# A graph network kernel on one core: the edges' states stay in SBUF from the first stage to the second attention

## What is computed

```python
h = relu(layernorm(x)) ; h = relu(h @ W_in + b_in)
for l in range(2):                       # L0: transformer convolution, 4 heads of 32
    res = h
    q, k, v = h@Wq[l]+bq[l], h@Wk[l]+bk[l], h@Wv[l]+bv[l];  e = edge_weight @ We[l]
    a   = softmax over the edges of one target of (q[dst] . (k[src]+e)) / sqrt(32)
    out = segment_sum((v[src] + e) * a, dst);  x_r = h @ Wskip[l] + bskip[l]
    b   = sigmoid([out, x_r, out - x_r] @ Wbeta[l]);  h = b*x_r + (1-b)*out
    h = relu(batchnorm(h)) + res         # statistics over all 50,000 nodes
x = x + h
# L1: for each edge an MLP of (x[src], edge_attr), mean over each target, then for each node an MLP
```

## Time and profile before

| | us |
|---|---|
| median of 3 runs | 2521.9 (2516.4 to 2528.1) |
| the profiled execution, whole | 2527.1 |
| the profiled execution, first to last instruction (its span) | 2525.3 |
| `first_layer_in` | 27 to 553 |
| `attention(0)` | 553 to 803 |
| `batch_norm_params(0)` | 803 to 814 |
| `dense_second` | 814 to 1212 |
| `attention(1)` | 1212 to 1567 |
| `dense_last` | 1576 to 2126 |
| `edge_last` | 2126 to 2525 |

### The profile page before, as it was taken

How to read it: one execution, slowest core, us unless ns; L and a number is a source line. 1 busy time by engine, 2 the same in 40 slices (tenths; PEclk the granted TensorE clock), 3 DMA queues, 4 the chain that set the end, 5 groups by cost and what they waited for, 6 DMA issues and landing times. The chain is left out here.

```text
span 2525.3 us, 38804 instructions
## 1 busy us (share of the span) xinstructions
PE 2013.4 (80%) x7514; PEld 1160.2 (46%) x7514; DVE 1733.3 (69%) x5020; ACT 1371.6 (54%) x2609; POOL 1290.4 (51%) x1119
## 2 busy tenths in 40 slices
PE   0898889879795777778366796499999995799997
PEld 0444444434232444444133232377777774466665
DVE  3899999965797777778422798477777773454552
ACT  0888888862121666666122221477667763556552
POOL 4645554418830333333587000677777763577773
PEclk9999999989797999999677798699999998899999
DMA  4778888859232999999544132999999993434440
GB/s 142 227 245 252 251 256 256 254 178 271 63 92 74 342 360 359 361 368 367 159 122 103 50 90 66 262 293 302 303 305 300 303 290 117 104 95 115 110 111 21
DMA packets 316448, 526.75 MB, mean 209 GB/s; under 512 B 87187, under 2 KB 189472, under 8 KB 316199
## 3 DMA queue, kind: packets, MB, share of 16 engines
q1 hardware_dynamic: 266100, 492.30, 61.5%
q0 software_dynamic: 46400, 33.03, 6.2%
q10 hardware_dynamic: 3824, 0.13, 0.1%
HBM read 304.11 MB, written 221.80 MB: 208 GB/s over the span
## 5 line engine op out<-in xcount | busy, mean ns | idle before, releaser
L476 POOL DMA_INDIRECT first_x<-in_x,first_index x200 | 254.5, 1272 | 230.1 <-ACT first_xn L339 140.8
L339 ACT ACTIVATE first_xn<-first_x,first_nb,first_rstd 125x128 f32<-125x128 f32 x600 | 245.4, 485 | 63.8 <-DVE first_nb L525 63.8
L795 POOL DMA_INDIRECT second_entry<-node_map,second_si x100 | 128.0, 1280 | 258.8 <-DVE second_src_row L808 221.0
L1086 PE MATMUL last_psH<-last_g,W2a 128*128 128x500 f32 x400 | 197.5, 618 | 31.9 <-DVE last_hid L1048 31.9
L868 PE MATMUL second_psZ<-second_h,gate_h 128*128 128x500 f32 x200 | 108.5, 624 | 112.8 <-DVE second_y L820 85.8
L1095 PE MATMUL last_psO<-W2b,last_hid 128*125 128x128 f32 x1600 | 193.3, 275 | 0.0
L1119 POOL DMA_INDIRECT elast_x<-x_rows,elast_si x100 | 138.6, 1386 | 99.8 <-issue 96.6
L1095 PEld LDWEIGHTS last_psO<-W2b,last_hid 128*125 128x125 f32 x1600 | 185.3, 190 | 0.9 <-issue 0.9
L585 PE MATMUL first_psZ<-first_h,gate_h 128*128 128x500 f32 x250 | 131.4, 607 | 47.6 <-DVE first_y L546 46.1
L339 ACT ACTIVATE last_xn<-last_x,last_nb,last_rstd 125x128 f32<-125x128 f32 x400 | 164.0, 486 | 0.1
L577 PE MATMUL first_psW<-first_h,W_in 128*128 128x500 f32 x300 | 157.6, 608 | 0.0
(11 more groups left out here) (260 smaller groups left out, 5326.1 us busy)
## 6 DMA issues: line engine op xcount, KB each, us to landing
hT<-first_h SPq DMA_DIRECT2D x100, 250.0 KB, 3.4
yT<-first_y SPq DMA_DIRECT2D x100, 250.0 KB, 3.5
second_yin<-yT SPq DMA_DIRECT2D x50, 500.0 KB
second_hin<-hT SPq DMA_DIRECT2D x50, 500.0 KB
yT<-second_y SPq DMA_DIRECT2D x50, 500.0 KB
last_yin<-yT SPq DMA_DIRECT2D x50, 500.0 KB
first_x<-in_x SPq DMA_DIRECT2D x100, 224.0 KB
h_rows<-second_rows SPq DMA_DIRECT2D x50, 448.0 KB
```

Of the source, the lines that this page charges most:

```text
L339: last = act.activation(xn[:, j], x[:, j], ACT.Relu, bias=nb[:, j:j + 1], scale=rstd[:, j:j + 1])
L476: pool.indirect_dma_start(x[:, to % X, j], None, a["x"], bass.IndirectOffsetOnAxis(index[:, end, r % 2, j:j + 1], 0), bounds_check=NODES - ...
L795: pool.indirect_dma_start(entry[:, q], None, scratch.node_map, bass.IndirectOffsetOnAxis(si[:, q], 0), bounds_check=NODES - 1, oob_is_err= ...
L1086: last = pe.matmul(psH[h][:, 0:CH], w.W2a[:, 0, h * 128:(h + 1) * 128], g[:, q % 2], start=True, stop=True)
```

## The change

1. Two tiles, `hd` and `hs`, 25 chunks each, are allocated once for `prepare` to `attention(1)`. `first_layer_in` makes the states of the edges' ends right in them and stores them no more; `attention` loads them no more. The map of node numbers (`ident_map`) lies in a part of `hd` until it is stored, so DVE waits once, at round 12, for that store.
2. `attention` writes `yd` over `hs[:, k]`, in place of the ring `yn`. `ydT` and `hdT` are stored in `attention(1)` alone, `hdT` in its query part, for `dense_last`.
3. In `attention`, what DVE made ahead of its first `product` is made in pieces between the products (`prepare(k)`, `count(k)`).
4. `dense_second` reads `yd` and `hd` in SBUF and updates `hd` in place; `load_edges` issues two DMAs, `store_edges` two. `load_edges(c)` waits for the statistics of edge chunk c-2. `ehw`, `eactw`, `eyw2` and `eywn` lie in `eyw`; `eact` and `esig` are single buffers.
5. The rings of `dense_second` shrink: `h2` and `rows` from eight chunks to four (two pairs), `y` from eight to six (three pairs); `yin` and `hin` stay at eight.
6. `dense_second` is written out without a loop (`unrolled`).

```diff
+def unrolled(n, ring, stages):
+    for t in range(n + max(lag for lag, _ in stages)):
+        for lag, stage in stages:
+            if 0 <= t - lag < n:
+                stage(t - lag, (t - lag) % ring, (t - lag) // ring)
...
@@ first_layer_in @@
+        def h1_of(k):
+            q, r = k % U, k // U
+            return h1[:, q] if q < DST else (edge.hd if q == DST else edge.hs)[:, r]
...
                 def store_h(k):
                     q = k % U
-                    table = scratch.hT if q < DST else scratch.hdT if q == DST else scratch.hsT
-                    hold(sp, ph.seen, *h1_made(k))
-                    sp.dma_start(cols_of(table, chunk(k)), h1[:, q]).then_inc(h1_stored[q], 16)
+                    if q < DST:
+                        hold(sp, ph.seen, *h1_made(k))
+                        sp.dma_start(cols_of(scratch.hT, chunk(k)), h1[:, q]).then_inc(h1_stored[q], 16)
...
@@ dense_second @@
-        h2 = ph.sb("h2", [128, U, CH])
-        rows = ph.sb("rows", [TILE, U, TILES, D])
+        h2 = ph.sb("h2", [128, 4, CH])
+        rows = ph.sb("rows", [TILE, 4, TILES, D])
-        y = ph.sb("y", [128, U, CH])
+        y = ph.sb("y", [128, 6, CH])
...
                 def load_edges(c, s, r):
-                    hold(sp, ph.seen, e.ywn, made(c - 2))
-                    sp.dma_start(eyn[:, s], cols_of(scratch.ydT, e_col(c))).then_inc(e_loaded[s], 16)
-                    sp.dma_start(ehd[:, s], cols_of(scratch.hdT, e_col(c))).then_inc(e_loaded[s], 16)
-                    sp.dma_start(eyw[:, s], cols_of(scratch.ywT, e_col(c))).then_inc(e_loaded[s], 16)
-                    sp.dma_start(econt[:, s], run_row(scratch.ct, e_col(c) + 1)).then_inc(e_loaded[s], 16)
+                    hold(sp, ph.seen, e.ywstats, made(c - 2))
+                    sp.dma_start(eyw[:, s], cols_of(scratch.ywT, at(c) * CH)).then_inc(e_loaded[s], 16)
+                    sp.dma_start(econt[:, s], run_row(scratch.ct, at(c) * CH + 1)).then_inc(e_loaded[s], 16)
                 def store_edges(c, s, r):
-                    hold(sp, ph.seen, e.hn, made(c))
-                    sp.dma_start(cols_of(scratch.hdT, e_col(c)), ehn[:, s]).then_inc(ehn_stored[s], 16)
                     hold(sp, ph.seen, e.rows, made(c))
...
                 def make_rows(k, q, r):
-                    act.wait_ge(rows_stored[q // 2], 16 * r + 16)
+                    act.wait_ge(rows_stored[k // 2 % 2], 16 * (k // 4) + 16)
...
                 def make_h2(k, q, r):
-                    dve.wait_ge(m.xz, made(k - U))
+                    dve.wait_ge(m.xz, made(k - 4))
+                    dve.wait_ge(m.turned, made(k - 4))
...
                 def make_y(k, q, r):
-                    dve.wait_ge(m.ystats, made(k - U))
-                    dve.wait_ge(y_stored[q // 2], 16 * r + 16)
+                    dve.wait_ge(m.ystats, made(k - 6))
+                    dve.wait_ge(y_stored[k // 2 % 3], 16 * (k // 6) + 16)
...
                 def edges_h(c, s, r):
+                    dve.wait_ge(e.bnw, made(c))
+                    dve.tensor_tensor(eyw[:, s], eyw[:, s], hd[:, at(c)], ALU.add).then_inc(e.hw, 1)
                     dve.wait_ge(e.bn, made(c))
+                    dve.wait_ge(e.hw, made(c))
+                    dve.tensor_tensor(hd[:, at(c)], eact[:], hd[:, at(c)], ALU.add).then_inc(e.hn, 1)
...
@@ attention, SP @@
-                    sp.dma_start(hd[:, k], cols_of(scratch.hdT, k * CH)).then_inc(in_loaded[q], 16)
-                    if l == 0:
-                        sp.dma_start(hs[:, k], cols_of(scratch.hsT, k * CH)).then_inc(in_loaded[q], 16)
+                def store_hd(k):
+                    sp.dma_start(cols_of(scratch.hdT, k * CH), hd[:, k]).then_inc(hd_stored, 16)
-                steps(C, [(0, load_index), (0, load), (0, load_weights_wide)])
+                steps(C, [(0, load_index), (0, load_weights_wide)] + [(0, store_hd)] * l)
-                steps(C, [(0, load_weight), (0, load_cont), (4, store)])
+                steps(C, [(0, load_weight), (0, load_cont)] + [(4, store_yd)] * l)
...
@@ attention, DVE: one piece of the former preparation behind each product @@
+                    elif 10 <= k < 15:
+                        c = 5 * (k - 10)
+                        after(dve.tensor_tensor(sel[:, c:c + 5], w.blocks[:].rearrange("p (o m) -> p o m", o=1).to_broadcast([128, 5, 128]),
+                                                ind[:, c:c + 5].rearrange("p (c o) -> p c o", o=1).to_broadcast([128, 5, 128]), ALU.mult))
-                steps(C, [(0, product)])
+                steps(C, [(0, product), (0, prepare)] + [(0, count)] * l)
```

More of the change, by code:

```diff
@@ L455, in _ @@
                     sp.wait_ge(xd_stored[s], 16 + 32 * len(range(s, ECHUNK, 2)))
[L456 to L459, removed]
+                for sems in (h1_stored, y_stored):
+                    for stored in sems:
+                        sp.wait_ge(stored, 16 + 16 * rounds)
             @block.gpsimd
@@ L692, in dense_second @@
         m = Group(**{n: ph.stage(n + "_made") for n in "si row bn h2 turned rows xz sig y ystats".split()})
-        eyn, ehd, eyw, econt, eyb, eact, eactw, ehn, ehw, esig, eyw2, eywn = (ph.sb(n, [128, 2, CH]) for n in (
-            "eyn", "ehd", "eyw", "econt", "eyb", "eact", "eactw", "ehn", "ehw", "esig", "eyw2", "eywn"))
+        eyw, econt, eyb = (ph.sb(n, [128, 2, CH]) for n in ("eyw", "econt", "eyb"))
+        eact, esig = ph.sb("eact", [128, CH]), ph.sb("esig", [128, CH])
+        hd, yd = edge.hd, edge.hs
         erows = ph.sb("erows", [TILE, 2, TILES, D])
-        e_loaded, ehn_stored, erows_stored = ph.loaded("e_loaded", 2), ph.stored("ehn_stored", 2), ph.stored("erows_stored", 2)
+        e_loaded, erows_stored = ph.loaded("e_loaded", 2), ph.stored("erows_stored", 2)
         e = Group(**{n: ph.stage(f"edge_{n}_made") for n in "yb bn bnw hn hw turned rows xz sig yw2 ywn ywstats init".split()})
-        e_col = lambda c: (ECHUNK - 1) * CH - c * CH
+        at = lambda c: ECHUNK - 1 - c
         def edges(stage, unit=4):
             def step(k, q, r):
-                if q % unit == 0:
-                    stage(2 * r + q // unit, q // unit, r)
+                if k % unit == 0:
+                    c = k // unit
+                    stage(c, c % 2, c // 2)
             return step
@@ L737, in store_edges @@
+                    sp.dma_start(econt[:, s], run_row(scratch.ct, at(c) * CH + 1)).then_inc(e_loaded[s], 16)
                 def store_edges(c, s, r):
-                    hold(sp, ph.seen, e.hn, made(c))
-                    sp.dma_start(cols_of(scratch.hdT, e_col(c)), ehn[:, s]).then_inc(ehn_stored[s], 16)
                     hold(sp, ph.seen, e.rows, made(c))
-                    move_rows(sp, rows_of(scratch.h2, NODES + (ECHUNK - 1) * CH - c * CH), flat(erows, s), erows_stored[s])
-                pipeline(sp, NCHUNK // 2, U // 2, [(0, load), (2, edges(load_edges, 2)), (5, store_rows), (6, edges(store_edges, 2)), (6, store_y)])
+                    move_rows(sp, rows_of(scratch.h2, NODES + at(c) * CH), flat(erows, s), erows_stored[s])
@@ L744, in _ @@
+                unrolled(NCHUNK // 2, U // 2, [(0, load), (2, edges(load_edges, 2)), (5, store_rows), (6, edges(store_edges, 2)), (6, store_y)])
                 for s in range(2):
-                    sp.wait_ge(ehn_stored[s], 16 + 16 * len(range(s, ECHUNK, 2)))
                     sp.wait_ge(erows_stored[s], 16 + 32 * len(range(s, ECHUNK, 2)))
@@ L1178, in attention @@
         o, sig, dx = (ph.sb(n, [128, 2, CH]) for n in ("o", "sig", "dx"))
-        yn = ph.sb("yn", [128, U, CH])
+        yd = edge.hs
         kj = dx
@@ new lines, in count @@
+                def count(k):
+                    nonlocal before
+                    if k == 15:
+                        after(dve.memset(ex[:], 1.0))
+                        after(dve.tensor_tensor_scan(fwd[:], cont[:, 0:CH], ex[:], 0.0, ALU.mult, ALU.add))
+                    elif k == 16:
+                        before, _ = across(fwd, zsum, through, ALU.add)
+                    elif k == 17:
+                        after(dve.scalar_tensor_tensor(out=run[:], in0=hflag[:], scalar=before, in1=fwd[:], op0=ALU.mult, op1=ALU.add))
+                        dve.reciprocal(bwd[:], run[:]).then_inc(counted, 1)
```

221 lines of the change are left out of this document (109 added, 112 removed).

## The result

The changed kernel takes 2497.9 us (median of 6 runs, 2492.5 to 2507.2), the kernel before beside it 2521.3 (6 runs, 2515.8 to 2528.1): 0.9909 of its time, 95% interval 0.9888 to 0.9930. That is 23 us less; the forecast was 2481.5, 40 less, in a range of 2455 to 2515. The profiled execution took 2495.5 us, with a span of 2493.8, and it is 31.5 shorter than the profiled one of before, which was a long one of its kind.

The account below looks back on a forecast made before the run. It took DVE to bound the first stage, PE attention 0, the transfers the second stage, and POOL's gathers attention 1's query part. Terms -8.5 - 1.5 - 29 - 1.4 = -40.4 from the median 2521.9 gave 2481.5, range 2455 to 2515.

Parts of the forecast that it names:

- First stage, 0: First stage: 50 stores leave the queue, 35 us of DMA time, but the queue was not the limit; gain 0.
- Attention 0's start, -8.5: Start of attention 0: the first product comes at 561.4 instead of 569.91, with DVE's preparation behind the products; -8.5 us.
- End of attention 0, -1.5: End of attention 0: the next phase no longer waits for the last yn store to land; -1.5 us.
- Removed transfers: Second stage: three transfers fewer per edge chunk lower the DMA floor of a four-chunk period from 15.55 to 13.4 us.
- Smaller rings: Second stage: DVE waits for the y store, so the period is 14.4, not 13.4 us; -29 us in 25 periods.
- landing at 7.7: Second stage: the y store lands 7.7 us after SP's hold for the edge loads ends, with 1.79 MB to carry.
- other bound: Second stage: seven SP issues done at 2.6 us after the hold, so a lone y store lands at 6.8.
- The stall only moves: Rival, second stage: the y store lands at about 8.9, the period stays 15.55; total -11.4 us, 2510.5; chance 0.19.
- slower: Rival, second stage: the y store meets today's queue, the period is 16.6; total +15 us, 2537; chance 0.10.
- Start of the second stage, -1.4: Start of the second stage: two loads fewer ahead of the first econt, 0.7 us each; -1.4 us.
- Attention 1, 0: Attention 1: POOL's gathers set the pace and wait for neither the loads nor the stores that replace them; 0.
- The loop: Second stage without a loop: gain at most 5 us; rival that straight code costs enough to cancel the gain, chance 0.04.

Follow-up runs that it names:

- either edit: Changed kernel with a y ring of four pairs (2469.3 us), or with SP's edge-chunk loads queued behind the same step's stores in the second stage (2464.6 us).
- the swap: Changed kernel with the y store ahead of the edge rows' store on SP's queue in the second stage, edge loads still first: 2495.7 us, 0.9888 of before.
- stores_first: Changed kernel with the edge-chunk loads behind the same step's stores on SP's queue in the second stage: 2464.6 us, 0.9756 of before.

## Why the prediction was right or wrong

1. *First stage, 0.* Not contradicted: the profiles' 5.6 us are within what one and the same stage varies by, and over twelve profiles the stage ends no earlier without the stores. The whole-kernel comparison alone would not exclude a few us.
2. *Attention 0's start, -8.5.* Right: from POOL's memset to the first product 6.8 us (549.14 to 555.90), where before it is 15.1 (554.85 to 569.91), so -8.3. The first wide edge weight landed within 3.7 us of its issue (552.16), predicted 3.4. The runs showed that both parts of the edit are needed for it: either alone leaves it at 10.9 or 14.4.
3. *End of attention 0, -1.5.* Right: 3.15 to 1.39, -1.8.
4. *Removed transfers.* Right in kind, and near in size. With a ring of four pairs they give 1.5 us in the mean period, and the limit that they leave is 13.46 to 13.67 by that mean, predicted 13.4. The prediction's number is one of the steady part, though. There (ends of L851 or its like from 850 to 1160 us) the periods are 15.6 before and 13.6 to 13.8 with either edit, so 1.8 to 2.0 of the predicted 2.15: the rest of the bytes did not pass at 363 GB/s, as the sum had it, but at 345 to 349.
5. *Smaller rings: the step that failed.* The mechanism was right, to the waiting instruction and the store that it waits for; the term was mis-sized. For "landing at 7.7" the two periods above have 9.5 and 8.6, and the mean of the 20 is 8.9: 1.2 us of error in one landing, 25 times, took all of the 29 us. The sum assumed "that at that period the queue runs empty for 1 us in each, so what stands ahead of the store is what was issued since 0". The runs show some 0.31 MB still in the queue at 0, which moves that bound to 8.6. The prediction's other bound failed too: "they are done at 2.6, and a lone 0.51 MB store would land 4.1 later, at 6.8" took the seven issues at 0.35 us each, and they took 4.2, so this bound lies at 8.3, above the other's 7.7. Either error alone would have used up half or more of the 29 us (15 for 8.3, 22 for 8.6, as estimates). Their shares are not separated: the swap took the issue's lateness away and left the queue's. The rival *The stall only moves* had the landing (8.9) and the period (unchanged), and one of the two causes (leftovers of `load(s)`); it had 0.19. It is what happened in this stage. The Trainium skill (DMA: Bandwidth & Descriptors, latency and other measured facts), on which the prediction said that by the loaded case the landing would be later than 7.7, agrees with these runs in direction. The fixed cost of about 2.0 us that the prediction also takes from it stands there for DMAs that GpSimd issues, and these stores are SP's; it gave a landing of 7.0, further from the measured 8.9 than the 7.7 from rows.
   The *slower* rival's period of 16.6 for "the y ring at today's queue" was measured when today's transfers stayed: 16.73. It was right as a statement on the kernel before, and would have been the result had the three transfers stayed.
6. *Start of the second stage, -1.4.* Right: from DVE's memset to the first scan it takes 830.4 - 813.94 = 16.5 before and 810.2 - 795.48 = 14.7 after, -1.8.
7. *Attention 1, 0.* Wrong in favour of the change, by 3.9 at its start: from POOL's memset to the start of ACT's first `hs` it takes 1212.08 - 1196.47 = 15.6 us, before 1236.45 - 1216.99 = 19.5. "the gathers set the pace and wait for neither" holds for loads and stores, but not for DVE: beside the instruction that makes `sel` a gather takes 3.77 us instead of 1.27, and this instruction is now in five pieces. Over the whole of attention 1 the profiles show some 3 us beside the luck of the clock.
8. *The loop.* Right: nothing.

Measured terms: -8.3 - 1.8 + 0.4 - 1.8 - 3.9 = -15.4, against 23 in the medians (0.4 is 364.6 - 364.2, the second stage's 24 periods). Of the 31.5 us between the two profiles, 5 more are attention 1 behind its last gather, where the changed kernel's profile had the better clock, and 5.6 the first stage; both are what a stage differs by from run to run. The rest of the 23 stays open. The change was faster by more than 0.5%, as forecast; the forecast time was 16 us too low. It lies in the range since that was drawn past the moved stall (2510.5), not since the forecast's path came true: the largest term, -29, came to nothing, and what lies between 2510.5 and the measured 2497.9 is attention 1's part and the open rest, which no term had.

## What to carry to other kernels

Where a change takes transfers away and pays for their room with shallower rings, cost the two against each other as a square of four cases: here both were worth 1.5 us a period and cancelled, and a further 33 us were to be had by letting the stores go ahead of the held load. A ring's depth is to be judged with the issue queue: look for the hold that stands in front of the store that frees the buffer, start the sum with what the queue still holds at that moment, not with an empty one, and take the time of the issues from a stretch as loaded as the one in question. A change that moves nothing in a stage may still have removed its old limit, so look whether the waits have a new name before the edit is written off.

## What the hardware did that was not expected

Gathers on POOL (`DMA_INDIRECT`) are held up by one long DVE instruction. In the kernel before, at the start of attention 1:

```profile
1227.75 1.27 POOL L1119 DMA_INDIRECT att_rows<-h_rows,att_idx  x1 [0.30 <-issue]
...
1228.46 3.49 DVE L1410 TENSOR_TENSOR att_sel<-blocks,att_ind 128x3200 f32<-128x3200 f32 x1
1229.33 3.77 POOL L1119 DMA_INDIRECT att_rows<-h_rows,att_idx  x1 [0.30 <-issue]
```

The gather of 3.77 us lies beside the 128x3200 product; the two before it take 1.27. With this product in pieces of 128x640 no gather is over 1.8 us in the changed kernel (2.2 in its variants), and with it in one piece in the changed kernel one takes 4.39 again, so the DVE instruction is shown as the cause, not the queue's load. Attention 0 has the same: POOL's indirect store to `node_map` that starts 0.12 us after `sel` of the earlier trace rows takes 4.44 us, and with the product in pieces the changed kernel's longest is 1.98. The Trainium skill (SBUF — State Buffer, "SBUF: two separate sides") says that a DVE instruction with two SBUF inputs holds a port pair, for the whole instruction, against a GpSimd instruction that reads SBUF. The trace agrees in kind: `sel` is made from two tiles, the gather takes its row numbers from a third (`att_idx`), and it ends 1.15 us after `sel` does, 1229.33 + 3.77 = 1233.10 against 1231.95. That the port is the reason no run here shows.

The share of time in which the DMA engines are busy is a poor measure of what they could still move: 4 points more of it came with 9% more bytes. The changed kernel has a share of 0.95 at 320 GB/s from 850 to 1150 us, `stores_first` 0.99 at 349, and the kernel before 1.02 at 363.

An issue on SP's queue isn't of a fixed price in code without a loop: from 850 to 1150 us of the changed kernel the same line takes 0.35 us and up to 1.5 us (`yT<-second_y`, least 350 ns, median 483, greatest 1502). It is not only the load of the DMA engines: in the emptiest period above, with 184 GB/s from 964.62 to 968.85, one issue of edge rows (L149) took 1.56 us.
